# GpSimd's gathers and scatters in rows of four, unrolled, with indices read straight from the table

## The chip, the cores and the metric

The kernel runs on one core of one Trainium2 chip. The metric is device time in microseconds, lower is better. A difference of 0.2% or less counts as none here.

## The reference, cut to what matters

The reference is one layer of a graph network with a residual and a layer norm. There are 50,000 nodes with 128 features each (32 scalars and 32 vectors of three), and 50,000 edges, sorted by receiver. The receivers are drawn as 50000·u², so low nodes have many edges (the lowest has 208) and high nodes few.

```
xs, xv = up-projection of s and v of each node
ss, vv = xs[senders], xv[senders]
w      = MLP(radial basis of edge length): 8 -> 64 -> 64 -> 128, silu between
m0..m3 = w * (ss, ss*Y1, vv, vv.Y1)                     # per edge
msg    = segment_sum([m0,m3],[m1,m2], receivers)        # scatter-add over nodes
out    = layernorm(x + out_projection(msg) / 16)        # per node
```

## The kernel before, in words

An array `acc` in HBM starts as a copy of x (80 pieces of 625 rows, highest nodes first, issued by SyncE at L297). Messages are added to it by indirect DMAs, and finished rows are read back in chunks of 1664 rows, normalised and stored.

Edges are worked on in 98 units of four tiles of 128 edges. A unit's four tiles are taken from two neighbouring rows of 512 edges (`turns` and `row_tiles`, L274 to L280), and units run from the highest receivers down. For each tile GpSimd issues one gather of the senders' rows of x into `sender` (L444) and, six units later (`LAG` = 6), one scatter with addition of `msg` into `acc` (L462). GpSimd builds the descriptors of both in software. A gather's buffer is one of `RING` = 4 slots and is free when TensorE has transposed the unit that used it (`senderT_ps`).

Between gather and scatter of a unit, TensorE transposes the senders (L527), projects them up (L548), computes the edge weights (L534 to L556), sums edges with the same receiver inside a tile (L568) and projects out (L580). VectorE forms the products and the row to scatter to (L900 to L961): only the first edge of a receiver in a tile goes to the real row; the others go to dump rows behind N. ScalarE copies the projected message into one of four `msg` slots (L668), after the scatters that used the slot have landed.

GpSimd's stream before is a loop of four steps (L478). One step issues gather i of unit s and scatter i of unit s−6 alternately, for i = 0 to 3. The indices of a step lie in a small double buffer, `index_now`, that a copy on GpSimd fills in the middle of the step before (L425). Two scatters that may touch the same row of acc must not be in flight together. So a scatter always waits for the landing of the scatter two before it (L454 to L456), and for the one just before it if a table (`scatter_orders`, made by VectorE in `make_scatter_orders`) says that the two tiles' ranges of receivers meet (L458). The first three steps always wait for the one before (L460). A value load at the start of a step (L432) reads the table's word for the unit, from which the number of acc pieces that must have been copied is worked out too (L433, L434).

SyncE reads a finished chunk when the scatters of a pair of units have landed (`landed`, L337); it doesn't hold GpSimd.

Of the kernel before, what the change touches and what calls it, by code (L numbers as in the profile page):

```python
# [20 lines left out]
I32 = mybir.dt.int32  # L21
# [3 lines left out]
P = 128  # L25
# [9 lines left out]
G = 4  # L35
# [6 lines left out]
RING = 4  # L42
STATS_AFTER = 4
# [4 lines left out]
SPARE = 3 * P  # L48
# [12 lines left out]
assert UNITS % 2 == 0 and LAG % 2 == 0 and UNITS <= P and FULL == UNITS - 1 and FULL >= 96  # L61
# [3 lines left out]
def bass_gnn(nc, x, src, dst, edge_vec, edge_len, W_up0, W_up1, w0, b0, w1, b1, w2, b2, W_out0, W_out1, out):  # L65
# [5 lines left out]
    with ctx:  # L71
# [13 lines left out]
        dump_row = sb("dump_row", [P, 2], I32)  # L85
        dump_rowf = sb("dump_rowf", [P, 2])
# [26 lines left out]
        meet = sb("meet", [1, TILES])  # L113
        meet_too = sb("meet_too", [1, TILES])
# [4 lines left out]
        orders = sb("orders", [1, UNITS])  # L119
# [14 lines left out]
        index = sb("index", [P, UNITS + LAG, 2, G], I32)  # L134
# [8 lines left out]
        index_now = sb("index_now", [P, 2, 2, G], I32)  # L143
        sender = sb("sender", [P, RING, G, D])
# [62 lines left out]
        pool_staged = sem("pool_staged")  # L207
# [76 lines left out]
        def _(sp):  # L284
# [100 lines left out]
        def _(pool):  # L385
# [3 lines left out]
            pool.iota(dst_raw[96:UNITS, :, :], [[0, G], [1, P]], base=N + 2 * P, channel_multiplier=0).then_inc(cleared, 1)  # L389
# [3 lines left out]
            pool.iota(dump_row[:, :], [[P, 2]], base=N, channel_multiplier=1).then_inc(cleared, 1)  # L393
# [11 lines left out]
            pool.memset(meet[:, :], 0.0)  # L405
# [11 lines left out]
            def stage(s, b, gathers=True, scatters=True, reused=True):  # L417

                if reused:

                    pool.wait_ge(gathered[b], 8 * G * ((min(s, UNITS) if isinstance(s, int) else s) - b))
                if scatters:
                    pool.wait_ge(rows_ready, s - LAG + 1)
                first, last = (0 if gathers else 1), (2 if scatters else 1)
                pool.tensor_copy(index_now[:, b, first:last, :], index[:, bass.ds(s, 1), first:last, :]  # L425
                                 .rearrange("p s a i -> p (s a) i")).then_inc(pool_staged, 1)

            def step(s, slot, gathers=True, scatters=True, reused=True, loop=True, following=None):
# [8 lines left out]
                if gathers and reused:  # L437
                    pool.wait_ge(senderT_ps, s - RING + 1)
# [627 lines left out]
```

## Time and profile before

| | |
|---|---|
| time, three runs | 1347.39, 1347.60, 1348.72 us (median 1347.6) |
| profiled execution: first to last instruction (its span; the page gives no other time of it) | 1340.7 us |
| GpSimd (POOL) busy | 1046.8 us, 78% |
| TensorE busy | 977.7 us, 73% |
| VectorE, ScalarE busy | 688.6, 544.5 us |
| scatters, gathers on GpSimd | 392 + 392; 1.593 and 1.005 us each on average |
| DMA, mean | 97 GB/s |

The span is counted from the first to the last instruction on the core; the timed runs hold in addition what lies around it. Busy time of GpSimd for an indirect DMA is the building of its descriptors, not the transfer; the transfer's end is given separately as "to landing", counted from the start of the instruction.

### The profile page before, as it was taken

What the parts mean: (1) busy time and instruction counts of PE and PEld (TensorE: products, weight loads), DVE (VectorE), ACT (ScalarE), POOL (GpSimd) and SP (SyncE); (2) the same over time, 40 slices, a digit from 0 to 9 for tenths busy, and PEclk for the clock granted to TensorE, in tenths of its full rate; (3) what the DMA queues carried; (4) which work ended last, traced back from release to release, by engine and by line L of the source; (5) the groups of instructions that cost most, each with busy time, mean ns of one, the idle gap of its engine ahead of it and who ended that gap; (6) DMA issues with size and microseconds to landing.
All of it is one profiled execution on the core that took longest, in us unless ns stands there. A gap on an engine that the chain in (4) does not pass through costs nothing.

```text
span 1340.7 us, 26289 instructions
## 1 busy us (share of the span) xinstructions
PE 977.7 (73%) x6206; PEld 919.7 (69%) x6206; DVE 688.6 (51%) x2880; ACT 544.5 (41%) x1403; POOL 1046.8 (78%) x923
## 2 busy tenths in 40 slices
PE   2896777786868868877876777887788778777810
PEld 1795777776767758767776777777777777677710
DVE  5762443466465465465366456366456556545402
ACT  5342232254344434444444435435435444424401
POOL 6547888888888888888888888888888888788771
PEclk9896877878787877887787878787778787878765
DMA  5778853343543443453443443444444444443332
GB/s 154 194 179 189 191 109 62 69 92 41 141 92 41 120 113 41 92 123 59 91 117 67 91 107 75 92 92 90 92 92 90 92 92 91 90 91 67 66 32 64
DMA packets 82531, 130.06 MB, mean 97 GB/s; under 512 B 16168, under 2 KB 66891, under 8 KB 81232
## 3 DMA queue, kind: packets, MB, share of 16 engines
q0 software_dynamic: 68992, 51.43, 28.2%
q1 hardware_dynamic: 12888, 77.14, 17.0%
q10 hardware_dynamic: 632, 1.29, 0.3%
q14 instruction: 14, 0.11, 0.0%
q8 instruction: 5, 0.08, 0.0%
HBM read 78.31 MB, written 77.09 MB: 116 GB/s over the span
## 4 chain that ended last, share of the span: by engine, by line
issue 37%; POOL 28%; DMA 27%; POOLq 6%; SPq 1%; DVE 0%; ACT 0%; ACTq 0%; DVEq 0%
DMA acc<-msg,index_now 17%; POOL sender L444 17%; DMA acc<-in_x_dram 9%; POOL acc L462 8%; POOLq L432 3%; POOL index_now L425 3%; POOLq L433 1%; SPq L297 1%; POOLq L434 0%; POOLq L458 0%; ACT normed L720 0%; DMA total<-acc 0%; POOLq L425 0%; POOLq L461 0%; POOLq L478 0%
## 5 line engine op out<-in xcount | busy, mean ns | idle before, releaser
L462 POOL DMA_INDIRECT acc<-msg,index_now x392 | 624.6, 1593 | 151.9 <-issue 124.9
L444 POOL DMA_INDIRECT sender<-in_x_dram,index_now x392 | 394.1, 1005 | 111.5 <-issue 99.9
L527 PE MATMUL ps_sT<-ident,sender 128*128 128x128 f32 x392 | 83.1, 349 | 269.1 <-DMA sender<-in_x_dram,index_now 268.9
L580 PE MATMUL ps_msg<-outw,sumT 128*128 128x64 f32 x1568 | 254.8, 334 | 0.0
L568 PEld LDWEIGHTS ps_sum<-same,mid 128*128 128x128 f32 x1568 | 248.1, 233 | 9.4 <-DVE mid L960 0.8
L580 PEld LDWEIGHTS ps_msg<-outw,sumT 128*128 128x128 f32 x1568 | 253.6, 253 | 0.0
L527 PEld LDWEIGHTS ps_sT<-ident,sender 128*128 128x128 f32 x392 | 54.7, 174 | 288.6 <-DMA sender<-in_x_dram,index_now 288.5
L568 PE MATMUL ps_sum<-same,mid 128*128 128x128 f32 x1568 | 250.9, 313 | 0.7 <-DVE mid L960 0.7
L938 DVE TENSOR_TENSOR proj<-ps_up,vec_all 128x384 f32<-128x384 f32 x98 | 54.3, 554 | 370.5 <-PE ps_up L548 361.1
L659 ACT COPY sumT<-ps_sum 128x512 f32<-128x512 f32 x196 | 114.9, 586 | 243.6 <-PE ps_sum L568 243.4
L720 ACT ACTIVATE normed<-total,shift,rstd 128x128 f32 x391 | 156.9, 481 | 50.6 <-DVE shift L1011 45.0
L677 ACT COPY senderT<-ps_sT 128x512 f32<-128x512 f32 x98 | 57.1, 583 | 271.1 <-PE ps_sT L527 271.1
L945 DVE TENSOR_TENSOR wts<-ps_wts,bias 128x512 f32<-128x512 f32 x98 | 67.7, 691 | 187.7 <-PE ps_wts L555 184.0
L548 PE MATMUL ps_up<-up,senderT 128*128 128x128 f32 x784 | 159.3, 366 | 5.3 <-DVE mid L952 5.3
L548 PEld LDWEIGHTS ps_up<-up,senderT 128*128 128x128 f32 x784 | 135.5, 260 | 22.2 <-issue 16.4
L555 PE MATMUL ps_wts<-mlp,hid 128*128 128x128 f32 x784 | 104.6, 277 | 0.6 <-ACT hid L695 0.6
L974 DVE BATCH_NORM_STATS2 stats<-total 128x6 f32 x391 | 78.6, 277 | 48.7 <-DMA total<-acc 48.1
L555 PEld LDWEIGHTS ps_wts<-mlp,hid 128*128 128x128 f32 x784 | 96.2, 193 | 1.3 <-ACT hid L695 1.3
L668 ACT COPY msg<-ps_msg 128x128 f32 (+1 forms) x98 | 26.0, 265 | 170.8 <-PE ps_msg L580 161.4
L534 PE MATMUL ps_hid<-basisT,mlp 32*128 32x128 f32 x392 | 94.5, 377 | 0.8 <-ACT basisT L675 0.8
L911 DVE CUSTOM_DVE_ANT_0 junk<-same,earlier 128x128 f32<-128x128 f32 x392 | 91.3, 288 | 3.4
L425 POOL COPY index_now<-index 128x8 int32 (+2 forms) x104 | 75.8, 729 | 5.2 <-DVE index L780 3.4
(140 smaller groups left out, 1089.1 us busy)
## 6 DMA issues: line engine op xcount, KB each, us to landing
acc<-in_x_dram SPq DMA_DIRECT2D x80, 312.5 KB
total<-acc SPq DMA_DIRECT2D x30, 832.0 KB
out_dram<-normed SPq DMA_DIRECT2D x29, 832.0 KB
sender<-in_x_dram,index_now POOLq DMA_INDIRECT x392
acc<-msg,index_now POOLq DMA_INDIRECT x392, 3.4
out_dram<-normed ACTq DMA_DIRECT2D x1, 832.0 KB
vec_raw<-in_edge_attr_dram SPq DMA_DIRECT2D x1, 576.0 KB
dst_raw<-in_dst_dram SPq DMA_DIRECT2D x1, 192.0 KB
```

The source lines that it names most:

```text
L425: pool.tensor_copy(index_now[:, b, first:last, :], index[:, bass.ds(s, 1), first:last, :] .rearrange("p s a i -> p (s a) i")).then_inc(poo ...
L444: pool.indirect_dma_start(sender[:, slot, i, :], None, x, bass.IndirectOffsetOnAxis(ap=index_now[:, b, 0, i:i + 1], axis=0)).then_inc(gath ...
L462: pool.indirect_dma_start(acc, bass.IndirectOffsetOnAxis(ap=index_now[:, b, 1, i:i + 1], axis=0), msg[:, msg_slot, i, :], None, compute_op ...
L527: mm = pe.transpose(ps_sT[:, P * i:P * (i + 1)], sender[:, k % RING, i, :], ident[:, :])
L534: mm = pe.matmul(ps_hid[:, q, :], mlp0[:, q, :], basisT[:, b, :], start=True, stop=True)
L548: mm = pe.matmul(ps_up[:, i, :], senderT[:, b, P * i:P * (i + 1)], up[:, :], start=True, stop=True)
L555: mm = pe.matmul(ps_wts[:, i, :], hid1[:, b, P * (i // 2):P * (i // 2 + 1)], mlp2[:, i % 2, :], start=True, stop=True)
L568: mm = pe.matmul(ps_sum[r][:, i, h, :], mid[:, b, 2 * r + i, P * h:P * (h + 1)], same[:, b, 2 * r + i, :], start=True, stop=True)
L580: mm = pe.matmul(ps_msg[:, i, 2 * MUL * h:2 * MUL * (h + 1)], sumT[:, b, i, h, :], outw[:, h, :], start=True, stop=True)
L659: act.copy(sumT[:, b, 2 * r:2 * r + 2, :, :], ps_sum[r][:, :, :, :]).then_inc(sum_ready[r], 1)
L720: mm = act.activation(normed[0:parts, b, r, :], total[0:parts, quarter, r, :].rearrange("p b d -> p (b d)"), ACT.Identity, scale=rstd[0:pa ...
L911: mm = dve.tensor_tensor_reduce(junk[:, b, i, :], same[:, b, i, :], earlier[:, :], 1.0, 0.0, ALU.mult, ALU.add, count[:, b, i:i + 1])
```

## The change

GpSimd's stream is written out for all 98 units, without a loop. For each unit it issues four gathers of unit v+6 in a row and then four scatters of unit v. Each DMA takes its index column from the big table `index` directly, so `index_now`, its copy and its semaphore are gone. The value load stands between the gathers and the scatters. A unit's first scatter waits for the landing of all four scatters of the unit before. Inside a unit a scatter waits for the one before it only if one bit, for the whole unit, says that any two of its four tiles meet (units 0 and 1 always wait). `row_tiles` now gives a unit the planes w and w+2 of its two rows, so that two tiles of a unit are at least two apart in edge order. The sender buffer has eight slots (`SRING`) instead of four, TensorE's loop has eight units in its body, and ScalarE waits for all four scatters of a message slot's last use. Each of the four tiles of a unit has dump rows of its own.

```diff
-SPARE = 3 * P
+SRING = 8
+SPARE = (G + 1) * P
         def row_tiles(a, w):
-            return a[:, 2 * w:2 * w + 2, 0:UNITS].rearrange("p q (j r) -> p q j r", r=2)
+            return a[:, w:w + 3:2, 0:UNITS].rearrange("p q (j r) -> p q j r", r=2)
...
             def landed(j):
-                for b in range(2):
-                    for i in range(2, G):
-                        sp.wait_ge(scattered[b][i], 16 * j + 16)
+                for i in range(G):
+                    sp.wait_ge(scattered[1][i], 16 * j + 16)
...
+            def gathers(u):
+                if u >= 2:
+                    pool.wait_ge(gathered[u % 2], 16 * G * (u // 2))
+                if u >= SRING:
+                    pool.wait_ge(senderT_ps, u - SRING + 1)
                 for i in range(G):
+                    pool.indirect_dma_start(sender[:, u % SRING, i, :], None, x,
+                                            bass.IndirectOffsetOnAxis(ap=index[:, u, 0, i:i + 1], axis=0)
+                                            ).then_inc(gathered[u % 2], 16)
+            def scatters(v):
+                c = v % 2
+                order = pool.value_load(scatter_orders[0:1, v:v + 1], min_val=2, max_val=2 * PIECES - 1)
+                pool.wait_ge(acc_init[0], 16 * (order // 4) + 16)
+                pool.wait_ge(acc_init[1], 16 * ((order + 2) // 4))
+                meets = order % 2
+                pool.wait_ge(rows_ready, v + 1)
+                pool.wait_ge(msg_ready, v + 1)
+                if v >= 1:
+                    for i in range(G):
+                        pool.wait_ge(scattered[1 - c][i], 16 * ((v + 1) // 2))
+                for i in range(G):
+                    if i >= 1:
+                        if v >= 2:
+                            pool.wait_ge(scattered[c][i - 1], 16 * (v // 2) + 16 * meets)
                         else:
+                            pool.wait_ge(scattered[c][i - 1], 16)
+                    pool.sem_inc(pool_passed, 1)
+                    pool.indirect_dma_start(acc, bass.IndirectOffsetOnAxis(ap=index[:, v, 1, i:i + 1], axis=0),
+                                            msg[:, v % RING, i, :], None, compute_op=ALU.add
+                                            ).then_inc(scattered[c][i], 16)
             pool.wait_ge(index_in, 1)
+            for u in range(LAG):
+                gathers(u)
             pool.wait_ge(spare_rows, 16)
             pool.wait_ge(scatter_tables, 1)
+            for v in range(UNITS):
+                if v + LAG < UNITS:
+                    gathers(v + LAG)
+                scatters(v)
...
-                    for i in range(2, G):
+                    for i in range(G):
                         act.wait_ge(scattered[b][i], 8 * (v - b) - 8 * RING + 16)
...
             def make_scatter_orders():
+                at = 0
+                for apart in range(1, G):
+                    n = G - apart
+                    dve.tensor_tensor(meet[:, :, at:at + n], high[:, :, 0:n], low[:, :, apart:G], ALU.is_ge)
+                    mm = dve.tensor_tensor(meet_too[:, :, at:at + n], high[:, :, apart:G], low[:, :, 0:n], ALU.is_ge)
+                    at += n
+                link(mm)
+                link(dve.tensor_tensor(meet[:, :, :], meet[:, :, :], meet_too[:, :, :], ALU.mult))
+                link(dve.tensor_reduce(meet_unit[:, :], meet[:, :, :], AX_X, ALU.max))
```

## Rows read from the trace of the kernel before

**Rows 1.** The page's first part: busy us, share of span, count.
```profile
PE 977.7 (73%) x6206; PEld 919.7 (69%) x6206; DVE 688.6 (51%) x2880; ACT 544.5 (41%) x1403; POOL 1046.8 (78%) x923
```
**Rows 2.** The page's chain that ended last, shares by line.
```profile
DMA acc<-msg,index_now 17%; POOL sender L444 17%; DMA acc<-in_x_dram 9%; POOL acc L462 8%; POOLq L432 3%; POOL index_now L425 3%; POOLq L433 1%; SPq L297 1%; POOLq L434 0%; POOLq L458 0%; ACT normed L720 0%; DMA total<-acc 0%; POOLq L425 0%; POOLq L461 0%; POOLq L478 0%
```
**Rows 3.** Busy by stretch: PE, PEld, DVE, ACT, POOL, clock, DMA, GB/s.
```profile
111.83:1266.12 1154.29, 895.74 (x5602) 842.58 (x5601) 606.23 (x2575) 485.77 (x1264) 943.19 (x801) 0.78 0.44 92
1266.12:1314.78 48.66, 13.16 (x111) 12.61 (x109) 7.42 (x25) 6.41 (x14) 36.81 (x28) 0.66 0.36 33
1314.78:1340.70 25.92, 0.00 (x0) 0.00 (x0) 8.31 (x50) 5.60 (x14) 1.55 (x1) 0.50 0.23 73
```
**Rows 4.** Groups of GpSimd, 111.83 to 1266.1: busy, mean ns, idle before.
```profile
L462 POOL DMA_INDIRECT acc<-msg,index_now x356 | 568.1, 1596 | 114.9 <-issue 99.0 <-DMA acc<-msg,index_now 15.0 <-DMA acc<-in_x_dram 0.9
L444 POOL DMA_INDIRECT sender<-in_x_dram,index_now x356 | 357.1, 1003 | 96.2 <-issue 90.7 <-DMA acc<-msg,index_now 5.2 <-DMA acc<-in_x_dram 0.3
```
**Rows 5.** Timeline of GpSimd in the even run: start, duration, idle before.
```profile
602.00 0.99 POOL L444 DMA_INDIRECT sender<-in_x_dram,index_now  x1 [0.30 <-issue]
...
609.67 1.59 POOL L462 DMA_INDIRECT acc<-msg,index_now  x1 [0.30 <-issue]
610.70 0.76 POOL L425 COPY index_now<-index 128x8 int32 x1
611.62 1.01 POOL L444 DMA_INDIRECT sender<-in_x_dram,index_now  x1 [0.17 <-issue]
...
623.54 0.77 POOL L425 COPY index_now<-index 128x8 int32 x1
```
**Rows 6.** Timeline of GpSimd in the prologue: gathers in a row.
```profile
35.24 0.94 POOL L444 DMA_INDIRECT sender<-in_x_dram,index_now  x1 [0.30 <-issue]
...
42.82 0.94 POOL L444 DMA_INDIRECT sender<-in_x_dram,index_now  x1 [1.55 <-issue]
```
**Rows 7.** Timeline of GpSimd, last scatters, the first and last of 25.
```profile
1264.23 1.59 POOL L462 DMA_INDIRECT acc<-msg,index_now  x1 [0.30 <-issue]
...
1314.78 1.55 POOL L462 DMA_INDIRECT acc<-msg,index_now  x1 [0.95 <-issue]
```
**Rows 8.** L462's answers: 51 to 111.83 (two lines), even run, 1265 on.
```profile
L462 POOL DMA_INDIRECT acc<-msg,index_now x12: 1586/1588/1638, 52.8 to 109.9; - x12
DMA to landing us min/median/max: 3.8/4.4/4.9
...
DMA to landing us min/median/max: 3.2/3.4/5.6
...
DMA to landing us min/median/max: 3.2/3.2/3.4
```
**Rows 9.** Chain of waits, 1274 to 1290: behind a landing at 1276.28.
```profile
1276.34 0.54 issue
...
1276.90 0.19 issue
```
**Rows 10.** Chain, 1165 to 1175, and then GpSimd's timeline of the same stretch.
```profile
1171.39 0.57 issue
1171.95 0.05 POOLq L432
...
1172.54 0.99 POOL L444 DMA_INDIRECT sender<-in_x_dram,index_now  x1 [0.30 <-issue]
1173.84 1.59 POOL L462 DMA_INDIRECT acc<-msg,index_now  x1 [0.30 <-issue]
```
**Rows 11.** Timelines of ScalarE and VectorE, and a line of the waits.
```profile
610.76 0.27 ACT L668 COPY msg<-ps_msg 128x128 f32 x1 [2.79 <-PE ps_msg L580]
...
49.95 0.68 ACT L669 COPY msg<-ps_msg 128x384 f32<-128x384 f32 x1
...
28.94 0.37 DVE L814 TENSOR_SCALAR norm<-norm 128x392 f32<-128x392 f32 x1 [3.99 <-ACT norm L636]
...
PE ps_sT L527 <- DMA sender<-in_x_dram,index_now: 268.9, 77, 11.3
```

More of the change, by code:

```diff
@@ L60 @@
 RSQRT_BITS = float(0x5f3759df)
-assert UNITS % 2 == 0 and LAG % 2 == 0 and UNITS <= P and FULL == UNITS - 1 and FULL >= 96
+assert UNITS % 2 == 0 and LAG <= SRING and (UNITS - 2) % SRING == 0 and UNITS <= P and FULL == UNITS - 1 and FULL >= 96
 assert NORM_AFTER > STATS_AFTER and NORM_AFTER > RING // 2 and (UNITS - 2) % RING == 0 and CHUNKS % 2 == 0 and PIECES % 2 == 0 and N % PIECE == 0 and REST <= P
@@ L112, in bass_gnn @@
         high = sb("high", [1, UNITS, G])
-        meet = sb("meet", [1, TILES])
-        meet_too = sb("meet_too", [1, TILES])
+        meet = sb("meet", [1, UNITS, G * (G - 1) // 2])
+        meet_too = sb("meet_too", [1, UNITS, G * (G - 1) // 2])
         piece_int = sb("piece_int", [1, UNITS], I32)
@@ L131, in bass_gnn @@
         gap_all = sb("gap_all", [P, UNITS, G])
-        index = sb("index", [P, UNITS + LAG, 2, G], I32)
+        index = sb("index", [P, UNITS, 2, G], I32)
         vec_all = sb("vec_all", [P, TILES, 3])
@@ L141, in bass_gnn @@
         basis_all = sb("basis_all", [P, TILES, NB])
[L143 to L144 removed]
+        sender = sb("sender", [P, SRING, G, D])
         basis = sb("basis", [P, 2, G * NB])
@@ L415, in _ @@
                                base=0, pattern=[[-1, P]], channel_multiplier=1).then_inc(consts, 1)
[L417 to L426, printed above, removed]
@@ L468, in _ @@
             pool.wait_ge(index_in, 1)
-            stage(0, 0, scatters=False, reused=False)
-            for s in range(LAG):
-                step(s, s % RING, scatters=False, reused=s >= RING,
-                     following=dict(scatters=s + 1 >= LAG, reused=s + 1 >= 2))
+            for u in range(LAG):
+                gathers(u)
             pool.wait_ge(spare_rows, 16)
             pool.wait_ge(scatter_tables, 1)
-            rounds = -(-(LAG + 3) // RING), (UNITS - 2) // RING
-            for s in range(LAG, rounds[0] * RING):
-                step(s, s % RING, loop=s - LAG >= 3, following={})
@@ L478, in _ @@
-            with pool.Fori(*rounds) as j:
-                for slot in range(RING):
-                    step(RING * j + slot, slot, following={})
-            for s in range(UNITS - 2, UNITS + LAG):
-                step(s, s % RING, gathers=s < UNITS,
-                     following=dict(gathers=s + 1 < UNITS) if s + 1 < UNITS + LAG else None)
+            for v in range(UNITS):
+                if v + LAG < UNITS:
+                    gathers(v + LAG)
+                scatters(v)
         @block.tensor
@@ L602, in _ @@
             turn(0, 0)
-            for u in range(RING):
+            for u in range(SRING):
                 unit(u, u)
-            with pe.Fori(1, (UNITS - 2) // RING) as j:
-                for k in range(RING):
-                    unit(RING * j + k, RING + k)
+            with pe.Fori(1, (UNITS - 2) // SRING) as j:
+                for k in range(SRING):
+                    unit(SRING * j + k, SRING + k)
             unit(UNITS - 2, UNITS - 2)
```

67 lines of the change are left out of this document (9 added, 58 removed).

## The prediction

> **What bounds the kernel now.** I read the page's first part, then its chain, then the time by stage, then GpSimd's groups and timeline. GpSimd is busy 78% of a span of 1340.7 us, more than TensorE's 73% [rows 1]. The chain of waits runs through GpSimd too: gathers (L444), scatters (L462), their landings and its value loads [rows 2]. It also names the row copies into acc up to 162 us, but scatters run at full rate from 113 us on, while the copies still land, so I don't count those as a bound. I cut the span at GpSimd's own marks [rows 3]: before 111.83 a slow start, 111.83 to 1266.12 the even run of 89 units (copy count of L425), 1266.12 to 1314.78 the last six units' scatters without gathers, and 25.92 us behind the last scatter. TensorE waits 268.9 us for gathers [rows 11], so nothing but GpSimd sets the pace of the even run: 1154.29/89 = 12.97 us a unit.
>
> In the timeline [rows 5] a gather takes 0.99 us, a scatter 1.59, and 0.30 goes between any two; the index copy lies inside a scatter and costs 0.06 behind it (gap 1.59 → 611.62 is 0.36) and some 0.03 in the two that follow. 4 × (0.989 + 1.59 + 0.604) + 0.09 = 12.82 us: the even run without disturbance is 89 × 12.82 = 1141, and 13 us are extra. Of these 568.1 − 356 × 1.590 = 2.1 and 357.1 − 356 × 0.989 = 5.0 are instructions that ran long, and 114.9 − 356 × 0.302 = 7.4 are waits of scatters, mostly for the one two before [rows 4].
>
> **The change part by part.**
>
> *Order of the eight DMAs.* The trace has both runs. Gathers behind a gather take 0.94 [rows 6]; scatters behind a scatter take 1.55 [rows 7] against 1.59 behind a gather. The gap stays 0.30 in both. A unit becomes gathers 0.99 + 3 × 0.944 = 3.82, scatters 1.59 + 3 × 1.552 = 6.25, gaps 8 × 0.302 = 2.42: 12.49 us. That is 0.33 below 12.82, of which the copy is 0.09 and the six kept neighbours 0.25. I take that the eight descriptor builds read their indices from the wide table as fast as from the small one. Bounds: if the 0.04 a DMA isn't saved, 12.73; if the direct column gave more, nothing here shows more than 12.49 minus the 0.08 that the two changes of kind still cost.
>
> *Even run.* 89 × 12.49 = 1111.6, plus 7.1 for long instructions, which I keep. The waits I drop: within a unit there is no wait left when no two tiles meet. With 98 units of 512 sorted receivers, of which the lowest one has 208 edges, tiles two apart (256 edges) never share one, so the wait value is always already reached. A unit's first scatter needs all four of the unit before. The last of those starts at T and lands at T + 3.4, at worst 5.6 [rows 8]; from landing to a dependent start it takes 0.75 plus some 0.1 (0.54 push, 0.19 start) [rows 9]. Four gathers lie between: T + 1.85 + 5.03 = T + 6.9. Even the worst landing, T + 6.5, is hidden. So 1118.7 against 1154.3: −35.6.
>
> *Sequencer.* The value load and its arithmetic, two acc_init waits, rows_ready, msg_ready and four more waits now stand behind four gathers (0.94 of cover each), where they stood behind a scatter. They can only hide if the sequencer runs ahead. It does: at 1171.39 it pushes the fourth scatter of a step and at 1171.95 starts on L432, though that scatter starts at 1173.84 and its gather only at 1172.54 [rows 10]. It is two DMAs ahead. L432 to L441 take 1.1 us there; with 0.2 for four waits and 0.75 the first scatter could start 2.05 us behind the push of the last gather. Two ahead, that push comes when the second gather starts, 3.7 us before the engine is free. Cost 0; with no run-ahead it would be 2.05 + 0.55 − 1.24 = 1.4 a unit.
>
> *Unrolling, direct columns, no copy.* Registers for loop values go; the loop's branch (L478) sits in that same run-ahead, and the period across it (copy at 610.70 to 623.54, with the branch pushed at 613.7) is 12.84 [rows 5], the undisturbed value, so removing it gives 0. Straight code has to be fetched. The only unexplained hole in straight DMA code is 1.55 instead of 0.30 [rows 6]; at 0 to 1.25 us, once in six units, the cost is 0 to 20 us. I take 0, since the steps before 111 us are straight code too and show no regular hole. The Trainium skill (Runtime: NRT & Kernel Launch, Instruction fetch mechanics) says that fetch is sequential in blocks, mostly hidden, and that a taken branch out of the window stalls for a fetch. By it the removal of 22 branches would be a further gain; the trace disagrees for this loop, with no stall at the wrap.
>
> *SRING 8, all four semaphores for the message slot.* ScalarE writes a unit's message some 7.8 us behind the end of the gathers two units on (610.76 [rows 11] against 602.99 [rows 5]). The slot's old scatters now come behind those gathers and land at 0.3 + 3 × 1.86 + 3.4 = 9.3 us. ScalarE waits 1.5 us, TensorE follows. Both have room: TensorE waits about 3 us a unit for gathers, and the message isn't needed until four units later. Cost 0; if it had no room, 1.5 × 89 = 133 us. TensorE's loop body doubles; its idle time covers that.
>
> *Prologue.* Thirteen table operations instead of eleven, six of them on longer tables, before directions() add by my estimate under 1 us on VectorE (0.54 us was 391 numbers wide), hidden in its 3.99 us wait [rows 11]. The first message is complete at 50.63 (49.95 + 0.68) [rows 11]; before, gather and scatter 0 followed it, so the first scatter started at 52.83. Now the gathers are done and it starts at 51.5: −1.3. Then units 0 and 1 are serial inside, as three units were before. One serial step is 5.19 (52.83 to 109.94 in 11) [rows 8]. Unit 0's last scatter starts at 51.5 + 3 × 5.2 = 67.1; + 1.89 + 5.03 gives unit 1 at 74.0, its last at 89.6, unit 2 at 96.5, its end 7.45 later at 104.0. Before, that point was 111.83: −7.8 with the 1.3.
>
> *Last six units.* No gathers are left to hide the wait for a whole unit. Before, every scatter waited for the second before it: 1264.23 to 1314.78 is 50.55 us in 24 steps, 2.11 each [rows 7]. Now three of four steps take 1.855, the fourth 3.3 + 0.9 = 4.2: the first 4.2, five units of 9.77, and 5.57 make 58.6: **+8.0**. The work behind the last scatter is unchanged, 25.9 us.
>
> **Sum.** −7.8 − 35.6 + 8.0 = −35.4: span 1340.7 → 1305.3. The page gives the profiled execution's span only; the three timed runs (median 1347.6) lie 6.9 above it, and I keep these. Forecast **1312 us**, −2.6%.
>
> **Rivals.**
> (a) *The builds don't get shorter.* For: 0.94 was seen in the prologue alone, and the long instructions show that builds are disturbed by other work. Against: 1.55 holds for all scatters of the tail. Unit 12.73: +0.25 × 89 = +22, time 1334.
> (b) *Code fetch shows.* A hole of 1.25 us once in six units: +20, time 1332.
> (c) *Slower: the turn from gathers to scatters is exposed.* The sequencer isn't ahead when it meets the value load, because the queue of waiting DMAs fills with gathers or the wait for four landings stops it, and the turn costs a unit 1.4 us. Place: before the first scatter of each unit. 1312 + 89 × 1.4 = 1437; it turns the sign from 0.40 us a unit. For: so many waits stood behind a gather nowhere before. Against: two DMAs ahead [rows 10] and 3.7 us of room.
> (d) *Slower: scatters back to back clog the queue*, so that landing passes 6 us: each us beyond costs 89 us. The same scatters ran back to back in the tail with landing 3.2 to 3.4 [rows 8], against it.
> (e) *Nothing gained:* the saved time comes back as waits for late landings or for TensorE. Time 1347. TensorE's waits speak against it.
>
> **Chances.** Forecast's family 0.62, (a) 0.14, (b) 0.09, (c) 0.07, (d) 0.03, (e) 0.05. A difference below 0.2% (2.7 us) can't be told from none here. (a), (b) and the forecast are faster, 0.85; (e) is mostly same, 0.04, and the rest slower, 0.11. Range: below, the long instructions vanish (7) and the serial start runs 5 us better, 1299; above, (a) with part of (b), 1341.
>
> **What would show it.** The profile after: steady unit 12.5 us; gather mean 0.96 and scatter 1.56; gap 0.30 at the turn as well (1.0 or more means (c)); a hole of over 1 us at equal distances means (b); first scatter at 51.5, unit 3's gathers at 104; the last six units' steps in the pattern 1.86, 1.86, 1.86, 4.2; ScalarE's message copy waiting for scatters some 1 to 2 us a unit. I am wrong in substance if the even run is above 12.8 us a unit.

## The result, and the profile after

| | median us | runs |
|---|---|---|
| before | 1348.16 | 1347.39 to 1351.05, 4 |
| after | **1335.06** | 1333.42 to 1336.70, 4 |

The ratio is 0.9888 (95% interval 0.9856 to 0.9921), 13.1 us faster. The forecast was 1312 in a range of 1299 to 1341. The profiled execution took 1335.3 us over a span of 1333.5.

The page's first part after the change; it answers to [rows 1]:

```profile
PE 928.8 (70%) x6206; PEld 871.6 (65%) x6206; DVE 692.2 (52%) x2882; ACT 537.5 (40%) x1403; POOL 1014.3 (76%) x817
```

GpSimd lost 106 instructions and 32.5 us of work and is still the busiest. Its chain by line (page, part 4; answers to [rows 2]): the two DMA lines themselves now lead, the landings fell from 17% to 6%.

```profile
POOL acc L444 20%; POOL sender L420 7%; DMA acc<-msg,index 6%; DMA acc<-in_x_dram 5%; SPq L295 3%; PE ps_msg L553 2%; PE ps_sum L541 2%; ACT normed L693 2%; PE ps_wts L528 2%; POOLq L427 1%; PE ps_hid L512 1%; PE ps_dst L494 1%; PE ps_sT L500 1%; ACT hid L656 1%
```

The busy time by stretch, cut at the same marks as [rows 3] (unit 3's first gather, the end of unit 91's scatters, the last scatter); stretch, its length, then busy PE, PEld, DVE, ACT, POOL, clock, DMA share, GB/s:

```profile
0.00:118.30 118.30, 63.78 (x413) 59.44 (x414) 58.91 (x198) 42.22 (x99) 61.17 (x81) 0.76 0.56 144
118.30:1251.10 1132.80, 852.01 (x5695) 799.81 (x5695) 619.37 (x2614) 483.85 (x1279) 915.73 (x712) 0.86 0.47 97
1251.10:1307.45 56.35, 13.04 (x102) 12.36 (x101) 5.58 (x21) 5.86 (x13) 35.87 (x23) 0.62 0.29 27
1307.45:1333.50 26.05, 0.00 (x0) 0.00 (x0) 8.32 (x50) 5.60 (x14) 1.57 (x1) 0.50 0.24 74
```

This is the ledger of the whole case. Terms in us of span:

| stretch | before | forecast | after | after − before | after − forecast |
|---|---|---|---|---|---|
| prologue | 111.83 | 104.0 | 118.30 | +6.5 | **+14.3** |
| even run, 89 units | 1154.3 | 1118.7 | 1132.8 | −21.5 | **+14.1** |
| last six units | 48.7 | 56.7 | 56.35 | +7.7 | −0.3 |
| behind the last scatter | 25.9 | 25.9 | 26.05 | +0.1 | +0.1 |
| span | 1340.7 | 1305.3 | 1333.5 | −7.2 | +28.2 |

Two terms failed, by 14 us each. The time missed by 23.1 and not 28.2 because of a third slip: I added 6.9 us to the span, but a timed execution is only 1.7 to 2.0 us longer than its own span in the runs of this case. The profiled execution of before was a quick one, near 1342.5; 5.1 us of my sum were the difference between executions.

**Even run.** GpSimd's groups in 118.30 to 1251.1 (busy, mean ns, idle before), answering to [rows 4], and its timeline over one unit, answering to [rows 5]:

```profile
L444 POOL DMA_INDIRECT acc<-msg,index x356 | 564.8, 1586 | 108.5 <-issue 103.9 <-DMA acc<-msg,index 3.7 <-DMA acc<-in_x_dram 0.9
L420 POOL DMA_INDIRECT sender<-in_x_dram,index x356 | 351.0, 986 | 108.6 <-issue 101.9 <-DMA acc<-msg,index 6.4 <-ACT msg L642 0.3
```

```profile
603.35 1.02 POOL L420 DMA_INDIRECT sender<-in_x_dram,index  x1 [0.30 <-issue]
604.68 0.98 POOL L420 DMA_INDIRECT sender<-in_x_dram,index  x1 [0.31 <-issue]
605.97 0.95 POOL L420 DMA_INDIRECT sender<-in_x_dram,index  x1 [0.30 <-DMA acc<-msg,index]
607.22 0.94 POOL L420 DMA_INDIRECT sender<-in_x_dram,index  x1 [0.30 <-issue]
608.47 1.62 POOL L444 DMA_INDIRECT acc<-msg,index  x1 [0.31 <-issue]
610.39 1.58 POOL L444 DMA_INDIRECT acc<-msg,index  x1 [0.30 <-issue]
612.28 1.56 POOL L444 DMA_INDIRECT acc<-msg,index  x1 [0.31 <-issue]
614.14 1.58 POOL L444 DMA_INDIRECT acc<-msg,index  x1 [0.30 <-issue]
616.03 1.02 POOL L420 DMA_INDIRECT sender<-in_x_dram,index  x1 [0.30 <-issue]
```

A unit takes 12.68 us (616.03 − 603.35). The gap at the turn from gathers to scatters is 0.31, so no wait is exposed there. The first instruction of a row takes longer than its kind did in the alternating order (1.02 against 0.99, 1.62 against 1.59), and the second is only halfway down.

**Prologue.** Timelines of GpSimd, VectorE, ScalarE, TensorE and SyncE's queue (start, duration, idle before and its releaser):

```profile
46.88 0.95 POOL L420 DMA_INDIRECT sender<-in_x_dram,index  x1 [0.30 <-issue]
68.34 1.64 POOL L444 DMA_INDIRECT acc<-msg,index  x1 [20.51 <-ACT msg L642]
...
52.26 0.56 DVE L908 TENSOR_TENSOR proj<-ps_up,vec_all 128x384 f32<-128x384 f32 x1 [17.40 <-remote]
...
52.30 0.47 ACT L668 ACTIVATE hid<-ps_hid,bias 128x256 f32<-128x256 f32 x1 [8.84 <-remote]
...
66.69 0.69 ACT L642 COPY msg<-ps_msg 128x384 f32<-128x384 f32 x1
...
34.50 2.07 PE L521 MATMUL ps_up<-up,senderT 128*128 128x128 f32 x8
43.52 1.22 PE L512 MATMUL ps_hid<-hid,mlp 128*128 128x256 f32 x2 [6.94 <-issue]
...
21.33 38.53 SPq L295 DMA_DIRECT2D acc<-in_x_dram  x10
```

The 28 gathers are through at 47.8, as forecast. The first message is not: its last copy ends at 67.4, where it ended at 50.63 before [rows 11]. GpSimd stands idle for 20.5 us. TensorE's product for `proj` ended at 36.57 (34.50 + 2.07), and VectorE, with nothing else to do, began on it at 52.26. ScalarE's `hid` began at 52.30, though its matmul (line 512, 43.52 + 1.22) was done at 44.7. Both start within 0.04 us of each other, 3.2 us behind the last gather's data (49.05). The work isn't slow; the news of its end arrives late: in the trace the semaphore that VectorE waits for rises at 52.23, 15.7 us behind the product, and ScalarE's at 52.27. SyncE shows the same: from 21 to 60 us it got out 10 of its row copies, where it got out 20 before. This row of SyncE (`acc<-in_x_dram`, count in a window from 16 to 60 us) is the witness I use below. In the records behind it, SyncE's short instructions last 0.70 us or start 0.70 or 1.40 us apart in the hold-up, where they last 0.03 to 0.05 and start 0.06 to 0.09 apart otherwise. These are the "slow steps" of the expectations. Counted plainly, as instructions of SyncE that last 0.65 to 0.75 us, there are 182 in the changed kernel and 1 in the one before.

**Tail.** GpSimd's timeline at unit 91's last scatter and behind; answers to [rows 7]:

```profile
1249.24 1.57 POOL L444 DMA_INDIRECT acc<-msg,index  x1 [0.30 <-issue]
1253.37 1.55 POOL L444 DMA_INDIRECT acc<-msg,index  x1 [2.56 <-DMA acc<-msg,index]
1255.22 1.57 POOL L444 DMA_INDIRECT acc<-msg,index  x1 [0.30 <-issue]
```

Steps of 4.13 and then 1.85: from 1249.24 to 1307.45 it is 58.2 us, forecast 58.6, before 50.55.

### The profile page after: what moved, and what is told of

Its sections match the earlier page's. It is cut to its first block, busy times and chain, and to the rows that moved or that the text cites. A ratio compares the mean times of both kernels' runs of the same rounds, so it can differ in the third digit from the quotient of the medians.

```text
span 1333.5 us, 25760 instructions
## 1 busy us (share of the span) xinstructions
PE 928.8 (70%) x6206; PEld 871.6 (65%) x6206; DVE 692.2 (52%) x2882; ACT 537.5 (40%) x1403; POOL 1014.3 (76%) x817
## 4 chain that ended last, share of the span: by engine, by line
issue 31%; POOL 28%; DMA 11%; PE 8%; another core or an unknown queue 7%; SPq 5%; ACT 4%; POOLq 3%; ACTq 1%; DVE 0%; DVEq 0%
POOL acc L444 20%; POOL sender L420 7%; DMA acc<-msg,index 6%; DMA acc<-in_x_dram 5%; SPq L295 3%; PE ps_msg L553 2%; PE ps_sum L541 2%; ACT normed L693 2%; PE ps_wts L528 2%; POOLq L427 1%; PE ps_hid L512 1%; PE ps_dst L494 1%; PE ps_sT L500 1%; ACT hid L656 1%
## 5 line engine op out<-in xcount | busy, mean ns | idle before, releaser
L444 POOL DMA_INDIRECT acc<-msg,index x392 | 621.1, 1585 | 170.3 <-issue 111.0
L420 POOL DMA_INDIRECT sender<-in_x_dram,index x392 | 386.8, 987 | 123.5 <-issue 111.9
L528 PE MATMUL ps_wts<-mlp,hid 128*128 128x128 f32 x784 | 139.4, 335 | 104.9 <-ACT hid L668 100.6
L553 PE MATMUL ps_msg<-outw,sumT 128*128 128x64 f32 x1568 | 202.0, 285 | 2.3 <-ACT sumT L632 1.6
L553 PEld LDWEIGHTS ps_msg<-outw,sumT 128*128 128x128 f32 x1568 | 200.0, 206 | 3.2 <-issue 1.2
L528 PEld LDWEIGHTS ps_wts<-mlp,hid 128*128 128x128 f32 x784 | 126.6, 245 | 111.8 <-ACT hid L668 107.0
L512 PE MATMUL ps_hid<-hid,mlp 128*128 128x256 f32 x196 | 78.8, 490 | 150.2 <-ACT hid L656 110.1
L521 PE MATMUL ps_up<-up,senderT 128*128 128x128 f32 x784 | 131.9, 319 | 28.8 <-issue 10.4
L512 PEld LDWEIGHTS ps_hid<-hid,mlp 128*128 128x128 f32 x196 | 35.8, 228 | 162.6 <-ACT hid L656 118.6
L521 PEld LDWEIGHTS ps_up<-up,senderT 128*128 128x128 f32 x784 | 111.2, 219 | 43.1 <-issue 21.8
## 6 DMA issues: line engine op xcount, KB each, us to landing
acc<-in_x_dram SPq DMA_DIRECT2D x80, 312.5 KB
```

Source lines behind the costliest of these rows:

```text
L420: pool.indirect_dma_start(sender[:, u % SRING, i, :], None, x, bass.IndirectOffsetOnAxis(ap=index[:, u, 0, i:i + 1], axis=0)).then_inc(gat ...
L444: pool.indirect_dma_start(acc, bass.IndirectOffsetOnAxis(ap=index[:, v, 1, i:i + 1], axis=0), msg[:, v % RING, i, :], None, compute_op=ALU.add
L512: pe.matmul(ps_hid[:, 2:4, :], mlp1[:, :], hid0[:, k % 2, :], start=True, stop=True).then_inc(hid1_ps, 1)
L521: mm = pe.matmul(ps_up[:, i, :], senderT[:, b, P * i:P * (i + 1)], up[:, :], start=True, stop=True)
L528: mm = pe.matmul(ps_wts[:, i, :], hid1[:, b, P * (i // 2):P * (i // 2 + 1)], mlp2[:, i % 2, :], start=True, stop=True)
L553: mm = pe.matmul(ps_msg[:, i, 2 * MUL * h:2 * MUL * (h + 1)], sumT[:, b, i, h, :], outw[:, h, :], start=True, stop=True)
```

## The experiments

Kernels of one group ran on one chip; the groups ran on different ones. "Step" is the even run over 89, s0 the first scatter's start.

### Group 1: what is new about the row of gathers

**ahead4**: every indirect DMA waits until the fourth before it has landed. **ahead4_prologue**: the same for the gathers of units 0 to 6 alone.

```diff
+            def hold(sem_, value):
+                if len(issued) >= 4:
+                    pool.wait_ge(*issued[-4])
+                issued.append((sem_, value))
```

> The changed kernel, with a semaphore for each of a unit's four gathers, and each DMA of GpSimd waiting for the landing of the fourth DMA before it, so that at most four are pushed and not landed. Theory A (run-ahead): in the changed kernel GpSimd's sequencer pushes gathers without a stop, and while many are pushed, the other engines' semaphores and SyncE's instructions are slow (0.70 us a step from 20 to 52 us), so the first message comes at 67.4 us instead of 50.6. Then here the first scatter starts at 51 to 53 us, SyncE's 0.70 us steps are gone in the even run too, and the time falls by 13 to 17 us from the changed kernel's 1335 to some 1320. Rival B (index read from the wide table slows the others): first scatter at 68 us as before, time 1335. Rival C (chance of where code blocks are fetched): first scatter anywhere, steps stay.

> As ahead4, but only the first 28 gathers are held back; from the first scatter on, GpSimd's stream is as in the changed kernel. Theory A: first scatter at 51 to 53 us, time 1320 within 3 us, because in the even run the slow steps cost other engines time that GpSimd doesn't wait for; SyncE's 0.70 us steps stay in the even run. If the slow steps cost the even run as well, this one is slower than ahead4 by that. Rival B: 1335, first scatter at 68 us.

1341.70 us (ratio 0.9964, 0.9944 to 0.9984), s0 66.44, 12 copies of SyncE; and 1337.40 us (0.9928, 0.99 to 0.9955), s0 68.94, 10 copies. With at most four in flight the signals are held up all the same. A backlog of more than four gathers isn't the cause.

**small_index**: the prologue's gathers read their indices from a tile of 28 columns instead of the wide table.

```diff
-  bass.IndirectOffsetOnAxis(ap=index[:, u, 0, i:i + 1], axis=0)
+  bass.IndirectOffsetOnAxis(ap=index_first[:, G * u + i:G * u + i + 1] if u <= LAG else index[:, u, 0, i:i + 1], axis=0)
```

> The changed kernel, with the index columns of the first 28 gathers copied once into a small tile (128x28) and read from there; no other wait is added, so the run-ahead stays. Theory A: the slow steps from 20 to 52 us and the first scatter at 68 us stay (later by the copy, under 1 us), time 1335. Rival B (wide table): first scatter at 52 us, time 1320.

1337.26 us (0.9929, 0.9899 to 0.996), s0 69.18. The wide table isn't it.

**before_direct**: the kernel before, its six prologue steps with direct columns.

> The kernel before, with the first six steps' gathers reading their index column from the wide table; the copies and waits stay where they are, so the run-ahead stays at two. Theory A: no 0.70 us steps, first scatter at 52 to 53 us, time as before, 1348 within 2 us. Rival B: slow steps from 15 us on, first scatter late, time up to 15 us longer.

1350.01 us (1.0014, 0.9985 to 1.0043), s0 57.96 against 52.83. SyncE got out 20 copies and VectorE began on `proj` at 36.7, as in the kernel before, while the three unbroken rows of this group, on the same chip, had 9 to 12 copies and began at 52.4 to 52.8. So the hold-up goes with the unbroken row. The first scatter moved by 5 us here all the same; whether the chip or the direct columns moved it isn't separated.

### Group 2: the order, the pauses, the tail

**alternate_unrolled**: before, unrolled, direct columns, no copy, alternating order. **two_and_two**: after, with rows of two (two gathers, two scatters, twice a unit).

```diff
 scatters(v):  for i in range(G):
+                    if i == 2 and v + LAG < UNITS:
+                        gathers(v + LAG, 2, G)
 ...
-                    gathers(v + LAG)
+                    gathers(v + LAG, 0, 2)
```

> The kernel before, with GpSimd's stream written out for all units, index columns read directly and no index copy; the order stays one gather, one scatter, with the waits of before (four sender slots). It separates the order from the rest of the change. Theory D (gathers in a row hold up the other engines' semaphore signals and SyncE's steps until the row has ended; ahead4 showed that neither how many are pushed nor, with small_index, the index's place does it): nearly no 0.70 us steps in the even run, first scatter at 52 to 58 us. The even run costs 12.73 us (4 x (0.989 + 1.59 + 0.604)) plus some 0.15 for waits, 12.85 to 12.9 a unit, against 12.73 measured in the changed kernel and 12.97 before: time some 1338 to 1341. Rival (unrolled direct DMAs are what causes the slow steps): they stay as in the changed kernel, first scatter at 66 to 69 us, time 1350 or more.

> The changed kernel with a unit's order two gathers, two scatters, two gathers, two scatters; the first 24 gathers stay in a row. By the durations of the changed kernel (gather 1.02 behind a scatter, 0.98 as second; scatter 1.62 behind a gather, 1.58 as second) a unit is 4 x 1.00 + 4 x 1.60 + 2.42 = 12.82 us: even run 0.1 to 0.15 us a unit longer than the changed kernel's 12.73, and time 1344 to 1348, since the slow prologue stays. If the price of a change of kind were 0.04, as the prediction had it, a unit would be 12.57 + 0.1. Theory D: fewer 0.70 us steps in the even run than in the changed kernel's 198, first scatter at 66 to 69 us.

1343.81 us (0.9959, 0.9937 to 0.9981), step 12.89; and 1365.46 us (1.0134, 1.0105 to 1.0163), step 13.10: slower than before, where 1344 to 1348 was expected. GpSimd's timelines, alternating and then in twos:

```profile
604.43 0.99 POOL L435 DMA_INDIRECT sender<-in_x_dram,index  x1 [0.30 <-issue]
605.72 1.59 POOL L453 DMA_INDIRECT acc<-msg,index  x1 [0.30 <-issue]
607.61 0.98 POOL L435 DMA_INDIRECT sender<-in_x_dram,index  x1 [0.30 <-issue]
```

```profile
600.33 1.02 POOL L420 DMA_INDIRECT sender<-in_x_dram,index  x1 [0.31 <-issue]
601.65 0.99 POOL L420 DMA_INDIRECT sender<-in_x_dram,index  x1 [0.30 <-issue]
602.95 1.63 POOL L446 DMA_INDIRECT acc<-msg,index  x1 [0.31 <-issue]
604.88 1.59 POOL L446 DMA_INDIRECT acc<-msg,index  x1 [0.30 <-issue]
606.77 1.02 POOL L420 DMA_INDIRECT sender<-in_x_dram,index  x1 [0.30 <-issue]
```

Means over 88 units of the even run, by place in the row (us):

| order | gathers | scatters | eight builds |
|---|---|---|---|
| alternating | 0.989 | 1.597 | 10.34 |
| twos | 1.023, 0.990 | 1.631, 1.598 | 10.48 |
| fours (after) | 1.051, 0.985, 0.954, 0.955 | 1.641, 1.580, 1.562, 1.562 | 10.29 |

The means hold some long instructions; the medians of the same places are plainer. They are 0.985 and 1.59 in the alternating order; 1.022 and 1.626 in the first place of a row, of two or of four; 0.982 and 1.58 to 1.59 in the second; 0.947 and 1.56 from the third on. So each of the two DMAs just before that is of the other kind adds 0.03 to 0.04 us, and a longer row of the other kind adds no more. Rows of two therefore lose 0.14 us a unit against alternating, and rows of four win 0.05, not the 0.25 that I booked. The rest of the twos' loss is waiting: their scatters wait 0.17 us a unit beyond the plain gaps, the alternating ones 0.10. Their prologue is held up too (s0 66.21), the alternating one's half as much (60.86).

**drained**: in the prologue each of units 1 to 6 starts its gathers when the unit before has landed.

```diff
+                if 1 <= u <= LAG:
+                    pool.wait_ge(gathered[1 - u % 2], 16 * G * ((u + 1) // 2))
```

> The changed kernel, with the gathers of units 1 to 6 waiting for the landing of all gathers of the unit before, so that the row of 28 has a pause of some 2 us after each four. Theory D: signals are let through in the pauses, the first message is ready at 51 to 55 us, the first scatter follows at 52 to 58 us, and the time falls from 1336 by 10 to 16 us, to 1320 to 1326. Rival (a pause doesn't help, what counts is the number of gathers before the first scatter): first scatter at 66 to 72 us, time 1336 or more.

1333.18 us (0.9881, 0.9844 to 0.9918). Timelines of ScalarE and GpSimd:

```profile
49.44 0.66 ACT L644 COPY msg<-ps_msg 128x384 f32<-128x384 f32 x1
...
65.33 1.64 POOL L446 DMA_INDIRECT acc<-msg,index  x1 [0.31 <-issue]
```

The message is there at 50.1 instead of 67.4, with all the gathers, and SyncE gets out 19 copies: pauses let the signals through. (tail_pairs below has the changed kernel's unbroken row on the same chip, with the message at 65.7 and 9 copies.) The time doesn't follow, since the pauses stretch the gathers themselves until 65, and the scatter stands behind them.

**tail_pairs** was to free the wait for the last unit's fourth scatter by a bit.

> The changed kernel with two table columns more (do the last tile of a unit and the first two of the next meet), and in the last six units, where no gathers lie between, the first scatter of a unit waits only for the first three of the unit before, the third one for the fourth. The changed kernel takes 71 us from the last scatter of unit 91 to that of unit 97, in steps of 1.86, 1.86, 1.86, 4.12. Here the long step becomes 2.3 to 2.5: 7.9 to 8.1 a unit, and the last scatter comes 6 x 1.7 = 10 us earlier; time 1325 to 1327. Rival: the end is set by something else (a chunk's load or the message of the last units), then less than 4 us come of it.

1457.12 us (1.082, 1.0784 to 1.0855). Its waits:

```profile
POOL acc L449 <- DMA acc<-msg,index: 159.8, 72, 3.9
```

I had taken the wrong tiles for neighbours: tile 3 of an even unit and tile 1 of the next are neighbours, the bit was set where they shared a receiver, and it makes the scatters inside that unit serial: in 16 units of the even run, three waits of some 2.3 us each, 111 us. **spread_tail** (group 3) repeated the error for odd units alone, and took 1462.19 us (1.086, 1.0837 to 1.0883), with three such waits in each of the same 16 units, all of them odd.

> The kernel before this one in the list with the last units changed: in the last units with an odd number, the first and second scatter wait for the landing of the last unit's fourth scatter only if the unit's bit is set, and the bit takes in whether that tile shares rows with either of the two (in odd units alone, where the tiles are three and five apart in edge order; in even ones they are neighbours, and the full wait stays). The step from unit to unit in the tail was 1.86, 1.87, 1.86 and 4.12 us; three of the boundaries of 4.12 lose one step of about 1.9 us, 5.6 us in all, so a time of 1313 to 1317 (first scatter to last 1233.5). Rival (the column sets the bit, as it did with neighbours): the units with the bit set take about 16 us instead of 9.7 for their scatters, and the time is over 1350. Rival (the landing of the third scatter, not of the fourth, ends the wait only 0.5 us sooner): a gain under 2 us.

### Groups 3 and 4: pauses that cost nothing, bytes, and the chip

**spread**, again as **spread_again**: only units 4 and 5 wait, and unit 0's scatters come ahead of unit 6's gathers. **narrow_gathers**, again as **narrow_again**: the row unbroken, but the gathers of units 1 to 6 fetch 64 bytes a row, so the rest of these rows is zero and their messages are not the right ones; GpSimd sets the zeros first, which starts its gathers 1.6 us later. **after_again** and **before_again** are the two kernels unchanged.

```diff
 spread:
+                if u in (4, 5):
+                    pool.wait_ge(gathered[1 - u % 2], 16 * G * ((u + 1) // 2))
 narrow_gathers:
+                    n = 16 if 1 <= u <= LAG else D
-                    pool.indirect_dma_start(sender[:, u % SRING, i, :], None, x,
+                    pool.indirect_dma_start(sender[:, u % SRING, i, 0:n], None, x if n == D else short,
```

Group 3:

> The changed kernel; in the prologue the gathers of units 4 and 5 wait until those of the unit before have landed, and unit 0's four scatters come ahead of unit 6's gathers. The gathers' bytes and their number stay. Theory (while gathers follow one another without a pause, signals between the other engines arrive late, so the first message is late): the gathers of units 0 to 3 are over near 32 us, when TensorE begins; after that there are two pauses of 3 to 5 us, so the first message is there by 50 to 53 us and the first scatter starts at 52 to 54 us instead of 68.3. From there as in the changed kernel (first scatter to the last 1239.1 us, 26.1 us behind it), so a span of 1317 to 1320 us, a time of 1319 to 1322 and a ratio of 0.978 to 0.981. Rival (the first message is late for another reason, such as the first load of ScalarE's table or the copies from the queue of SyncE): the first scatter stays at 65 us or later and the time at 1332 to 1336. Rival (it is early, but the four scatters ahead of unit 6's gathers only bring forward a wait for acc's zeros): the first scatter at 53, unit 3's still after 120, time above 1330.

> The changed kernel; the gathers of units 1 to 6 (24 of the 392) fetch rows of 16 floats instead of 128 (64 bytes instead of 512) from the flattened x, so GpSimd builds as many descriptors, in the same row without a pause, and an eighth of the bytes moves; the rest of those tiles is zero, and their messages are not the right ones. GpSimd sets the zeros first, about 3 us. If the signals are held up by the bytes that the gathers move, the first message comes by 55 us and SyncE's steps of 0.70 us are gone before it. If they are held up by GpSimd's building or by the number of descriptors, the build stays 0.95 us, SyncE's slow steps stay from 20 to 50 us, and the first scatter starts at 67 us or later, as in the changed kernel.

> The kernel before, unchanged, once more, for the trace of another of its executions: their times were 1341 to 1354 us, and the profiled one was among the quickest. Theory (signals are held up now and then in its prologue too, where its gathers run with few pauses): an execution slower than the profiled one by x us has its first scatter later than 52.8 by most of x, with SyncE's steps of 0.70 us ahead of it, and 12.97 us a unit in the even run as before. Rival (the spread comes from the even run or from the tail): the first scatter at 52.8 and a step other than 12.97 us.

spread 1330.01 us (0.99, 0.9876 to 0.9924), s0 49.97; narrow_gathers 1325.26, s0 52.55; before_again 1350.03, s0 55.36, step 13.01 and a tail of 51.8. Its 7.6 us over the first profile are spread over prologue (3), even run (3) and tail (1), with no hold-up: my theory of before's spread was wrong. SyncE's queue in the three, in that order:

```profile
19.48 40.25 SPq L295 DMA_DIRECT2D acc<-in_x_dram  x20
```

```profile
19.48 39.91 SPq L296 DMA_DIRECT2D acc<-in_x_dram  x21
```

```profile
19.52 40.67 SPq L297 DMA_DIRECT2D acc<-in_x_dram  x20
```

All undisturbed. I would have read narrow_gathers as "it was the bytes". But the kernel before too was undisturbed here, and nothing said what the changed kernel itself does on this chip. So both went again beside it, as group 4.

> The changed kernel itself, once more, beside the spread and the narrow gathers on one chip. If the row of gathers holds up the signals wherever it runs: first scatter at 65 to 69 us, 190 to 210 steps of SyncE of 0.70 us, a time of 1333 to 1337. If it takes a chip on which this happens: either as above, or no such step, the first scatter at 50 to 53 us and a time of 1326 to 1331 (the spread one's 1330.0 then owes nothing to its pauses).

> The kernel with two pauses in the prologue's gathers and unit 0's scatters ahead of unit 6's gathers, once more. If the pauses are what lets the signals through: the first scatter at 50 to 54 us also where the unchanged row of gathers has it at 65 or later, and a time 5 to 10 us under the changed kernel's on this chip. If they do nothing: the first scatter as in the changed kernel on the same chip, to 3 us, and the same time within 3 us; on a chip without the slow steps it is even a little slower, since the first four scatters took 5 to 6 us each where nothing lay between them.

> The changed kernel with rows of 64 bytes instead of 512 in the gathers of units 1 to 6, once more, beside the changed kernel itself on this chip. Where the changed kernel has SyncE's slow steps ahead of its first scatter: if the bytes make them, they are gone there and the first message comes by 55 us; if the number of descriptors or GpSimd's building does, the first scatter is at 67 us or later. Where the changed kernel has none, this one has none either, and it tells nothing.

| group 4 | time us | s0 | step |
|---|---|---|---|
| after_again | 1334.01 (1333.26 to 1336.38) | 68.37 | 12.72 |
| spread_again | 1330.24 (1328.20 to 1331.44) | 55.82 | 12.73 |
| narrow_again | 1338.62 (one run) | 70.26 | 12.76 |

SyncE's queue and GpSimd's first scatter, for after_again, narrow_again and spread_again:

```profile
22.04 36.97 SPq L295 DMA_DIRECT2D acc<-in_x_dram  x9
...
68.37 1.64 POOL L444 DMA_INDIRECT acc<-msg,index  x1 [20.47 <-ACT msg L642]
```

```profile
20.70 39.42 SPq L296 DMA_DIRECT2D acc<-in_x_dram  x11
...
70.26 1.64 POOL L448 DMA_INDIRECT acc<-msg,index  x1 [20.69 <-ACT msg L648]
```

```profile
20.13 39.63 SPq L295 DMA_DIRECT2D acc<-in_x_dram  x18
...
55.82 1.64 POOL L446 DMA_INDIRECT acc<-msg,index  x1 [9.21 <-DMA acc<-in_x_dram]
```

An eighth of the bytes leaves the hold-up whole; two pauses take 12.6 us off the first scatter (68.37 to 55.82). Only 6.7 of these reach unit 3 (113.70 against 120.38), since gathers of two units then follow in one row behind unit 0, and the time falls by 3.8, less than expected. The same narrow kernel that was held up here was not in group 3, and the spread kernel has 144 of SyncE's instructions of 0.70 us here and 5 there. So the hold-up of the first message needs an unbroken row of gathers *and* a chip that shows it, though each narrow kernel is a single execution. Three of the four chips of the groups showed it, and so did the changed kernel's first profile.

One more thing in the traces goes with the chips. The page's last part gives the scatters a median time to landing in spread and none in spread_again, the same kernel:

```profile
acc<-msg,index POOLq DMA_INDIRECT x392, 3.3
```

```profile
acc<-msg,index POOLq DMA_INDIRECT x392
```

The time is there in before, before_again, spread, narrow_gathers and spread_tail, and it is missing in every other trace, the old order of before_direct included. Behind it, a trace should hold 6272 landing records of gathers: spread has 6260, the kernel before 6214, spread_again 1270 and the changed kernel 1128, missing over the whole run. So signals were held up only where most of these records are missing. Whether the recording of signals shares in the hold-up, or both have one cause, wasn't tested; an execution timed without it would be the test. What differs between the chips stays open, and so does what in GpSimd's work delays the signals. What is left of the hold-up in spread_again costs nothing that shows: 1330.24 us here, 1330.01 on the chip without it. What the changed kernel does on the chip of group 3 wasn't run; narrow_gathers, at 1325, is the nearest to it.

**spread_tail2**: spread, with a bit that is right about neighbours. In the last six units an odd unit's first scatter no longer waits for the even one's fourth, an even unit's first no longer for the odd one's third and fourth, unless the bit says so.

```diff
+                    for i in range(G):
+                        loose = last and i >= (3 if c else 2)
+                        pool.wait_ge(scattered[1 - c][i], full - 16 + 16 * meets if loose else full)
```

> The spread kernel with the waits of the last six units by which tiles can share rows at all. A unit's tiles are the places 0, -4, 2, -2 (in edge order, from the pair's first) in even units and 1, -3, 3, -1 in odd ones, and the next even unit's lie 8 lower; so only the tiles 0 and 2, and 1 and 3, of an even unit are neighbours of those of the odd unit behind it. In the last units, an odd one's first scatter waits for the even one's fourth only if the bit is set, its second in full; an even one's first waits for the odd one's third and fourth only if the bit is set, its third and fourth in full. The pairs of tiles that are let go are added to the bit. Steps between units in the tail: 4.12 us now; 2.3 in front of an odd unit, 1.87 in front of an even one: 3 times 1.86 and 3 times 2.25 less, 12.3 us. So the tail (first scatter of unit 91 to the last) 46 us instead of 58.2, and a time 10 to 13 us under spread_again's. Rival (the bit is set again): over 1350 us. Rival (third and second scatters land no sooner than the fourth, the queue being in order and late): under 4 us.

1318.17 us (1316.53 to 1320.12; 0.9797, 0.976 to 0.9834), 12.1 under spread_again. GpSimd's timeline over unit 92 and into 93:

```profile
1243.62 1.57 POOL L453 DMA_INDIRECT acc<-msg,index  x1 [0.31 <-issue]
1245.49 1.55 POOL L453 DMA_INDIRECT acc<-msg,index  x1 [0.30 <-issue]
...
1251.09 1.57 POOL L453 DMA_INDIRECT acc<-msg,index  x1 [0.30 <-issue]
1253.43 1.55 POOL L453 DMA_INDIRECT acc<-msg,index  x1 [0.78 <-issue]
```

1.87 in front of an even unit, 2.34 in front of an odd one; the tail (1243.62 to 1290.16) is 46.5 us, forecast 46. This version beats both kernels.

## Why the prediction was right and wrong

- *Prologue, "Now the gathers are done and it starts at 51.5": failed.* The gathers were done; the message wasn't. I took the first message's time from a trace in which the prologue's gathers had an index copy in every four and pauses of up to 1.6 us, and left it where it was, while closing those pauses. Measured 68.34, 16.8 late, of which the serial units gave 2.5 back: 14.3 us. Shown: the same message is at 50.1 with pauses (drained) and at 54.9 with two of them (spread_again), against 67.4. On one chip of four the first message wasn't late, so on such a chip this step might have held; the changed kernel wasn't run there.
- *Order, "gathers 0.99 + 3 × 0.944 = 3.82, scatters 1.59 + 3 × 1.552 = 6.25": failed in size.* Each row had the best-placed values from places where no other kind was near, and its first instruction at the alternating price. Measured 3.94 and 6.35, so 0.22 a unit too little, 20 us over 89; the 7.1 us that I had kept for long instructions are inside these means, which leaves 12.5. Gaps of 0.305 instead of 0.302, with rounding, add the 1.6 that make it 14.1. The saving of the even run, 21.5 us, is: unrolling and no copy 7.4 (12.97 to 12.89, another chip), and 14.1 from the order (12.89 to 12.73; drained, whose even run is the changed kernel's, took 12.73 on the chip of the 12.89). Of these, 0.05 × 89 = 5 are shorter builds and 9 are waits of scatters that are gone. The waits that I dropped are indeed 0: no gap in the changed kernel's even run is over 0.31.
- *Turn, sequencer, wide table, code fetch: right.* 0.31 us at the turn against rival (c), no hole against (b), and no wait for a landing over 0.31 us in the even run against (d). I had booked 0.09 × 89 = 8.0 for the copy and nothing for the loop, and alternate_unrolled, which drops both, gained 7.4. The Trainium skill (Runtime: NRT & Kernel Launch, Instruction fetch mechanics) lets a taken branch stall for a fetch only if its target lies outside a window of two blocks of 256 instructions. The loop's body is 114 instructions in the trace of before, so by the page too its branch costs no fetch, and I was wrong to read a gain out of it; the trace agrees, with no stall at the wrap. Rival (a) named my time, 1334, but not its reason: builds three and four did get shorter.
- *Tail, +8.0: right*, 7.7 to the last scatter; and it wasn't a price of the order but of a wait that half the tiles didn't need.
- *Message slot, "waits 1.5 us, cost 0": the cost was right, the wait was not.* ScalarE's wait line in the changed kernel is

```profile
ACT msg L641 <- DMA acc<-msg,index: 134.8, 39, 8.0
```

That would be 1.4 us a unit, but it names only 39 of 98 copies, at 3.5 us each, in a trace that lacks most landings. In spread, whose trace has them, ScalarE stands idle 442.1 us in front of 89 copies of the even run, 5.0 each, all ended by a landing; before it was 1.7, ended by the product. So the slot costs ScalarE about 3.3 us a unit. It costs the kernel nothing: GpSimd waits for no message after the prologue.
- *Base, "I keep these 6.9": failed*, by 5.1 us in the other direction.

## What to carry to other kernels

A time read from a trace belongs to the neighbours it had there: where an edit packs one engine's instructions closer, what other engines finished meanwhile has to be questioned too, by the first dependent step and not by the packed engine. Price an instruction by its place in the new pattern, not by the best place seen; where the pattern isn't in the trace, give both ends. And before an experiment's good value is credited to its edit, run the unedited kernel beside it on the same chip. And a line of waits that names few of an instruction's executions, in a trace that lacks landings, is not the whole of its waiting.

## What the runs showed of the hardware

- In the profiled executions, while GpSimd issues gathers without a pause, signals between other engines can arrive almost 16 us late and SyncE gets out 9 to 13 copies of 312.5 KB between 16 and 60 us instead of 19 to 21. VectorE's comes through about 3 us behind the row's last data. It takes neither many DMAs in flight (four suffice) nor many bytes (64 a row suffice). On one chip of four it didn't happen, and there the trace also holds nearly all landing records, which on the others it doesn't.
- In the even run of the changed kernel on the other chips SyncE's short steps are held up too, in 46 of the 89 units of the first profile, mostly from the second gather to the second scatter; it costs nothing (step 12.73 there, 12.75 for the same kernel on the chip without), since GpSimd waits for nobody.
- An indirect DMA of 128 rows of 512 bytes occupies GpSimd 0.95 us as a gather and 1.56 as a scatter-add where the two before it are of its own kind, 0.98 and 1.59 where one of them is not, and 1.02 and 1.63 where neither is (medians), with 0.305 between any two; with 64 bytes a row a gather still follows a gather every 1.25 us.
